# Batch 0's normalisation between layers one and two, moved into the last units of layer one and kept on chip; the first weights and rows of layer one split in pieces

## What is computed

```python
# layer one: attention over the 512 columns, 16 heads of 64, for each of 8 batches
h = concat(Wqkv0 @ z[:, :, :256] + Winj0 @ u[:, :, :256],
           Wqkv1 @ z[:, :, 256:] + Winj1 @ u[:, :, 256:])
q, k, v = split(h)
prob = softmax(((q + r_w_bias)^T k) / 8)
x = Wo @ (prob applied to v) + bo + z
m, var = mean(x, axis=1), var(x, axis=1)        # over the 256 rows
x1 = (x - m) * rsqrt(var + eps)
# layer two begins: normalisation along the 512 columns, then a recurrence
xa = (x1 - mean(x1, -1)) * rsqrt(var(x1, -1) + eps) * ln1_w + ln1_b
sx = shifted(xa) - xa
t = tanh((xa + sx * maa_x) @ maa_w1)            # then mixtures, v, g, k, r, the decay and the scan
```

## Time and profile before

| | |
|---|---|
| median of 3 runs | 3575.32 us (3566.74 to 3576.97) |
| the profiled execution's own time | 3579.84 us |
| its span in the profile | 3578.0 us |
| TensorE busy | 3336.2 us (93%) |
| VectorE busy | 2391.6 us (67%) |
| ScalarE busy | 1786.6 us (50%) |
| GpSimd busy | 193.4 us (5%) |
| DMA | 296.08 MB, mean 83 GB/s |

### The profile page before, as it was taken

One profiled execution on the slowest core, in us unless ns is written; L12 is line 12 of the kernel. 1 busy time (PEld: TensorE's weight loads), 2 busy tenths in 40 slices (PEclk: granted clock), 3 DMA queues, 4 the chain that ended last, 5 costly groups with the idle time before them and its releaser, 6 DMA issues. The chain is left out here.

```text
span 3578.0 us, 55148 instructions
## 1 busy us (share of the span) xinstructions
PE 3336.2 (93%) x21472; PEld 2557.2 (71%) x21472; DVE 2391.6 (67%) x3779; ACT 1786.6 (50%) x4253; POOL 193.4 (5%) x311
## 2 busy tenths in 40 slices
PE   7999999999999997689999999679999999699998
PEld 6777778887778875556666666357888777488885
DVE  5666666656666564399999999727777888642212
ACT  4444444444454443445655554327777777532222
POOL 0000000000000000000000000001110111000000
PEclk9999999999999998789999999779999999899999
DMA  4323311231122113354444444220011111220004
GB/s 177 118 107 130 118 72 71 89 124 71 71 95 83 71 71 117 80 117 101 105 109 113 107 107 105 55 106 1 25 40 65 48 42 37 69 71 24 24 12 160
DMA packets 93312, 296.08 MB, mean 83 GB/s; under 512 B 20000, under 2 KB 28192, under 8 KB 68480
## 3 DMA queue, kind: packets, MB, share of 16 engines
q1 hardware_dynamic: 64752, 186.47, 17.8%
q0 software_dynamic: 10368, 75.50, 5.6%
q10 hardware_dynamic: 17936, 30.59, 2.4%
HBM read 233.82 MB, written 58.72 MB: 82 GB/s over the span
## 5 line engine op out<-in xcount | busy, mean ns | idle before, releaser
L453 ACT ACTIVATE l_prob<-l_bank,l_nmax 128x512 f32<-128x512 f32 x512 | 344.9, 686 | 280.8 <-DVE l_nmax L539 280.8
L539 DVE TENSOR_REDUCE l_nmax<-l_bank 128x1 f32<-128x512 f32 x512 | 317.7, 683 | 68.4 <-PE l_bank L373 68.4
L339 PE MATMUL l_bank<-l_x_hi,l_w_hi 128*128 128x256 f32 x1024 | 297.7, 291 | 15.8 <-DVE l_x_lo L598 15.8
L562 DVE COPY l_probT<-l_bank 128x512 f32<-128x512 f32 x256 | 173.8, 689 | 178.0 <-PE l_bank L387 176.7
L339 PE MATMUL l_bank<-l_x_hi,l_w_lo 128*128 128x256 f32 x1024 | 290.8, 284 | 0.0
L339 PE MATMUL l_bank<-l_x_lo,l_w_hi 128*128 128x256 f32 x1024 | 290.7, 284 | 0.0
L1611 DVE TENSOR_TENSOR_SCAN l_kv<-l_wx,l_kv 128x2056 f32<-128x2056 f32 x64 | 283.8, 4435 | 1.9 <-DVE l_nrs L1624 1.8
L2179 ACT ACTIVATE l2a_sc<-l2a_sc,l2a_nmax 128x256 f32<-128x256 f32 x512 | 254.8, 508 | 41.1 <-DVE l2a_nmax L2295 41.1
L387 PE MATMUL l_bank<-l_ident,l_prob 128*128 128x128 f32 x2048 | 250.6, 278 | 15.2 <-DVE l_k_lo L555 10.6
L387 PEld LDWEIGHTS l_bank<-l_ident,l_prob 128*128 128x128 f32 x2048 | 229.0, 142 | 28.4 <-DVE l_k_lo L555 20.8
L409 PE MATMUL l_bank<-l_probT,l_v 128*64 128x512 f32 x1024 | 233.8, 598 | 0.0
(11 more groups left out here) (327 smaller groups left out, 8225.2 us busy)
## 6 DMA issues: line engine op xcount, KB each, us to landing
l_vb<-vd SPq DMA_DIRECT2D x64, 1024.0 KB
l_w_hi<-kept_w_hi POOLq DMA_DIRECT2D x24, 1024.0 KB, 8.2
l_w_lo<-kept_w_lo POOLq DMA_DIRECT2D x24, 1024.0 KB, 10.2
l_wv_hi<-kept_wv_hi POOLq DMA_DIRECT2D x12, 1024.0 KB, 5.1
l_wv_lo<-kept_wv_lo POOLq DMA_DIRECT2D x12, 1024.0 KB, 7.1
l_wraw<-in_l_wqk SPq DMA_DIRECT2D x8, 1024.0 KB, 8.4
kept_w_hi<-l_w_hi SPq DMA_DIRECT2D x8, 1024.0 KB, 10.9
kept_w_lo<-l_w_lo SPq DMA_DIRECT2D x8, 1024.0 KB, 12.5
```

What stands on the lines that cost most here:

```text
L339: mm = pe.matmul(s.ap[:, c * ROWS:(c + 1) * ROWS], a[:, kt, c, g, :], b[:, kt, c * ROWS:(c + 1) * ROWS], start=m == 0, stop=m == 3 * KT - 1)
L453: act.activation(prob[h][:, it, :], s.ap[:, :], ACT.Exp, bias=nmax[:, n % 2, it, h:h + 1], accum_out=rsum[:, n % 2, it, h:h + 1]).then_inc ...
L539: dve.tensor_reduce(nmax[:, n % 2, it, h:h + 1], s.ap[:, :], AX.X, ALU.max, negate=True).then_inc(max_ready, 1)
L562: dve.tensor_copy(probT[0][:, j, :], s.ap[:, :]).then_inc(s.drained, 1)
```

## The change

Thirteen small buffers of the normalisation (`an`, `x`, `own_rows`, `other_rows`, `ncol`, `bo`, `cb`, `eps`, `power`, `nrs`, `sm`, `sd`, `nb`) are allocated ahead of both layers and handed to both. Layer one makes batch 0's normalisation at the ends of its units 50 to 57: the bias product after unit 50, `centre_rows` and the two pairs of activations after 51, the variances after 52, the power on POOL in 53, the spreading and `scale_rows` after 54, the sums after 55, their power on POOL in 56, `normed` after 57. SP loads `bo` and `att[0]` after the last loads of `acc`, and stores x1 of batch 0 before the last two stores of `att`. Layer two starts with b = -1, so its first TensorE instruction is the transposes of batch 0, and loads `att[1]` in place of `att[0]`.

In layer one's start, the first weights and rows come as two halves (rows of `x`, then of `u`), each rounded and subtracted by itself; TensorE's q product starts when the first half is there and waits in front of its seventh matmul for the second. VectorE no longer waits for `rb` before the splits. In turn 0, `split_wv` moves from the lane-0 units of the odd pairs to the lane-1 units of the even pairs (units 2, 6, 10 to units 1, 5, 9).

```diff
-def l0_attention(nc, kept, d, x, u, att):
+def l0_attention(nc, kept, first, d, x, u, att, x1):
+    NORM = HALF - 14
+    BIAS, CENTRE, VAR, SPREAD, SUMMED, NORMED = NORM, NORM + 1, NORM + 2, NORM + 4, NORM + 5, NORM + 7
@@ order of the PSUM slots
+            order += {BIAS: ["cb"], CENTRE: ["nc_0", "nc_1"], VAR: ["nv"], SPREAD: ["nr"]}.get(n, [])
@@ SP, start and end of layer one
-                sp.dma_start(wraw[:, :, :, :, :], d["l0_wqk"][0]).then_inc(wraw_in, 16)
-                load_x(0, 0)
+                for h in H2:
+                    own = slice(h * RT, (h + 1) * RT)
+                    sp.dma_start(wraw[:, own, :, :, :], d["l0_wqk"][0][:, own, :, :, :]).then_inc(first_in[h], 16)
+                    sp.dma_start(xraw[:, own, :], (x, u)[h][0].rearrange("(r p) n -> p r n", p=P)).then_inc(first_in[h], 16)
...
+                sp.dma_start(bo[:, :], d["l0_bo"]).then_inc(bo_in, 16)
+                sp.wait_ge(acc_stored[0], 16)
+                sp.dma_start(an[:, :, :], att[0].rearrange("(r p) n -> p r n", p=P)).then_inc(an_in, 16)
+                sp.wait_ge(x1_ready, 1)
+                sp.dma_start(x1[0].rearrange("(r p) n -> p r n", p=P), xf[:, :, :]).then_inc(x1_stored, 16)
                 for l in range(LANES):
                     store_acc(TURNS - 1, l)
@@ TensorE
+                    if n == 0:
+                        pe.wait_ge(first_lo, 2)
...
+                            if n == 0 and name == "q" and c == 0 and m == 3 * RT:
+                                pe.wait_ge(first_lo, 4)
...
                     turn_probs(n)
                     turn_sums(n)
+                    if n == BIAS:
+                        bias_rows()
+                    if n == CENTRE:
+                        centre_rows()
+                    if n == VAR:
+                        column_variances()
+                    if n == SPREAD:
+                        spread_deviations()
@@ ScalarE
                     sums(n)
+                    if n == BIAS:
+                        bias_rows()
+                    if n == CENTRE:
+                        centred()
+                    if n == SUMMED:
+                        moments()
+                    if n == NORMED:
+                        normed()
@@ VectorE
-                dve.wait_ge(rb_in, 16)
-                split_w(0)
-                split_x(0, 0)
+                for h in H2:
+                    own = slice(h * RT, (h + 1) * RT)
+                    dve.wait_ge(first_hi, 2 * h + 1)
+                    dve.tensor_tensor(w_lo[0][:, own, :, :, :], wraw[:, own, :, :, :], w_hi[0][:, own, :, :, :].bitcast(F32),
+                                      ALU.subtract).then_inc(first_lo, 1)
...
+                dve.wait_ge(rb_in, 16)
                 split_wv(0)
...
                     if bp == 0 and l == 0 and pair + 1 < HP:
                         split_w(pair + 1)
-                        if pair % 2 == 1:
-                            split_wv((pair + 1) // 2)
+                    if bp == 0 and l == 1 and pair % 2 == 0 and pair + 2 < HP:
+                        split_wv(pair // 2 + 1)
...
                     probs(n)
+                    if n == VAR:
+                        column_deviations()
+                    if n == SPREAD:
+                        scale_rows()
@@ layer two
-    ALL = range(-2, B + 1)
+    ALL = range(-1, B + 1)
...
-                load_att(0)
-                sp.dma_start(bo[:, :], d["l0_bo"]).then_inc(bo_in, 16)
                 sp.dma_start(vec[:, :, :], d["l1_vec"]).then_inc(first_in, 16)
                 sp.dma_start(w1[:, :, :], d["l1_w1"]).then_inc(first_in, 16)
                 load_before(0)
+                load_att(1)
...
-                pe.wait_ge(consts, 2)
-                bias_rows()
+                pe.wait_ge(consts, 1)
...
-                        pe.wait_ge(xn_ready, p + 1)
+                        if p:
+                            pe.wait_ge(xn_ready, p)
```

More of the change, by code:

```diff
@@ new lines, in normed @@
+                def normed():
+                    act.wait_ge(x1_stored, 16)
+                    act.wait_ge(dev_ready, 1)
+                    for r in range(RT):
+                        ins = act.activation(nb[:, r:r + 1], nb[:, r:r + 1], ACT.Copy, scale=sd[:, r:r + 1])
+                    ins.then_inc(nb_ready, 1)
+                    act.wait_ge(nb_ready, 1)
+                    for r in range(RT):
+                        act.activation(xf[:, r, :], xf[:, r, :], ACT.Identity, bias=nb[:, r:r + 1], scale=sd[:, r:r + 1]).then_inc(xn_ready, 1)
@@ L742, with l1_layer @@
 MIX = ["w", "k", "v", "r", "g"]
-def l1_layer(nc, d, att, x1, u, vd, x2):
+def l1_layer(nc, first, d, att, x1, u, vd, x2):
     HS, NJ, PER, CG = 16, 8, 8, 32
```

209 lines of the change are left out of this document (150 added, 59 removed).

## The result

| | before | changed |
|---|---|---|
| median | 3572.51 us (3566.74 to 3576.97, 4 runs) | 3537.59 us (3535.91 to 3546.13, 4 runs) |
| ratio to before | | 0.9908, 95% interval 0.9895 to 0.992 |
| the profiled execution's own time | 3579.84 us | 3535.91 us |
| TensorE busy | 3336.2 us | 3319.9 us |

The change saves 34.9 us by the medians. A second study later gave the changed kernel 3537.57 (ratio 0.9899, 0.9882 to 0.9915).

The account below looks back on a forecast made before the run. It took TensorE to bound layer one and a chain of short steps to bound the gap behind it. -5.5 - 6.9 + 8.4 - 28.7 = -32.7 from 3575.3 gave 3542.6, rounded 3543; range 3530 to 3557.

Parts of the forecast that it names:

- the case that was given 0.62: The prediction's main case for the whole kernel: 3543 us, with its own bounds giving 3535 to 3552.
- The start, -5.5: Layer one's start: loading and splitting first weights and rows in halves saves 5.5 us, bounds 4 to 6.5.
- The first half takes the place of the 1 MB that landed by 5.62: Layer one's start: the first halves of weights and rows, together 1 MB, land by 5.62 us.
- I take half of each: Layer one's start: half-width rounding and subtraction take half of 1.91 and 2.29 us.
- its two readings of the clock: Layer one's start: clock rises 5.9 us after the first product, gain 6.1; or counted anew after the pause, gain 4.8.
- The splits, -7: Turn 0 of layer one: one split per unit instead of two saves 2.3 us per group, 6.9 over three groups.
- 1.4 us lost for one of lateness: Unit 2 of layer one: TensorE loses 1.4 us for each microsecond that `k_lo` comes late.
- rival C: Units 50 to 57: inserted waits over 4 us let TensorE's clock fall, giving 3587 us; chance 0.02.
- Added to layer one, +8.4: Layer one's late units: 7.4 us of added products plus 1.0 of stall, bounds 7.4 to 14.
- length less 2.4: Layer one: work ahead of the exponentials costs TensorE its length less 0.96 + 1.5 = 2.4 us.
- The gap, -28.7: Between layers one and two: first product with a weight at 1417.6 instead of 1446.27, saving 28.7 us, bounds 20 to 32.
- Until then its own ten issues: Layer two's start: ScalarE is busy with ten load issues until `w1` lands at 1410.8.

Follow-up runs that it names:

- the squares twice: The changed kernel with only the two squares of batch 0's sums repeated on ScalarE ahead of unit 56's exponentials; 3539.2 us (one time).
- the issues moved: The changed kernel with ScalarE's ten issues of layer two's later constants behind first_part of batch 0 instead of at its start; 3532.6 us (one time).
- the sums twice: The changed kernel with all sums of batch 0's x1, on ScalarE between units 55 and 56, made twice; 3544.3 us (one time).

## Why the prediction was right, and where it was off

The forecast was 3543, measured 3537.6, inside the range and in the case that was given 0.62. Of the 5.4 us between them, 2.8 are the level of before (3575.3 in the runs shown, 3572.5 with a fourth), 2.2 the sum, -34.9 against -32.7, and the rest rounding. That the sum came so close is in part luck: the start was put 1.6 us too high and the splits 2.1 too low, and the two cancel.

- **The start, -5.5: -3.9.** The mean of v's first product is 23.6 over the three runs with the old start and 19.7 over the eight with the change's. This is just outside the bounds of 4 to 6.5. Three steps failed. "The first half takes the place of the 1 MB that landed by 5.62": it landed at 6.43 to 6.75, the second at 9.14 to 9.86. "I take half of each" for half the width: 1.06 and 1.23, where half of 1.91 and 2.29 is 0.96 and 1.15. So the first product came at 10.03 to 10.34, forecast 9.0. And of its two readings of the clock the dearer is the right one: with a pause in front of the seventh product the half clock lasts 2.9 to 5.9 us counted from the restart, 5.5 to 8.5 from the first product; without a pause it is 2.7 to 5.9 (each to the first record under 0.36 us). That 5.9 us, the longest of the starts without a pause, was taken for the length hid that this part varies by 3 us from run to run. The Trainium skill says in the place that the prediction named ("TensorE: Matmul & The Clock Gate", on the clock's states) that the ramp differs between runs of one kernel; the thirteen profiles agree. Whether it is a budget of time and not of matmuls they can't decide, since at half clock the products stand 0.21 us apart in all of them; either has to be counted from the restart, where the prediction's 6.1 counted through the pause.
- **The splits, -7: -9.0.** That a single split is hidden for the most part was seen rightly (it costs 0.55 where 1.0 was forecast), but "1.4 us lost for one of lateness" read a fall of the clock as a slope. The rival C of the prediction priced just this mechanism, and looked for it in the new units alone, while it was at work in unit 2 of before: the term failed by a wait of 2.86 us followed by a granted 0.50.
- **Added to layer one, +8.4: +7.8.** Each product cost a little less than its row: 0.79, 3.43, 1.69, 0.90, against 1.0, 3.5, 1.9 and 1.0. The wait of unit 56 is 0.95, forecast 1.0; `centred`, `normed` and `scale_rows` were hidden, as said: units 54 and 57 are unchanged, unit 52 is longer by less than its products. The law "length less 2.4" gives 2.5 for the run with the squares twice, measured 0.95 + 1.54 = 2.49.
- **The gap, -28.7: -29.4.** The size was right and the limit not, so the size owes something to luck. "Until then its own ten issues" stood in the text as cover of `w1`; they were the limit by 1.2 us, and `w2b` came at 1411.7, in time for the product at 1412.7. The run with the issues moved shows it. Counted from layer one's last VectorE operation, `w1` and `w2b` landed at 8.3 and 15.0 where the prediction's numbers give 9.9 and 16.6, and the issues, until 9.4, took up most of the difference.
- **The rest of the layers.** Layer two's scans start 33.2 us nearer to layer one's end in this pair of profiles, where some 29 were forecast; the 3.8 beyond the gap are spread of the prologue. This prologue, from the first product with a weight to the first scan, took 56.9 to 64.4 us in the eleven profiles with the old order of v's loads, with no relation to the edits that these show (the same changed kernel took 58.1 and 62.0): in the longest (the sums twice) the granted clock is 0.54 from 10 to 20 us behind the first product, where the start alone has 1.00. From the first scan to the last VectorE operation it took 2064.9 in before and 2058.4 in the changed kernel, over the 5 us by which the prediction would have called itself wrong; but the kernel with the start alone, which has none of the moved work, took 2058.4 too, and that with the squares twice 2064.4. So these 6.5 us can't be put down to the moved work, and two single profiles of this kernel can't be subtracted to better than some us.
- **Rival C.** It was to decide from 6.4 us of ScalarE's work ahead of the exponentials. With 6.5 the clock fell, with 4.9 it didn't, and between them nothing was tried; the change's 3.35 stay clear. What it priced at 2.9 more than the wait cost 2.1, and it needed no 4 us of idle time in the record: 2.7 were enough, and in unit 63 even 2 in some executions.

The sum with the measured terms: -3.9 - 9.0 + 7.8 - 29.4 = -34.5, against -34.9 from the medians.

## What to carry to other kernels

A chain of short steps between two stages can be worth moving into a stage whose bound engine takes it at the bare length of its products; price each product by the distance of starts at full clock, and the other engines' share by the spare time ahead of the bound engine's next need. Before a stall is given a slope, look at the granted clock behind it: a long wait of TensorE (here from about 2 us on, in some executions) costs its length and more, so two extras on a helper engine are best put in different units. And once a chain is cut, look at what its first engine itself does before its first step, its own DMA issues included, and at loads queued behind a wait that they do not need.

## What the runs showed of the hardware

- TensorE's clock fell to half behind eight waits of 2.86 us, one of 3.22 and one of 2.73, and did not behind 0.66, 1.02 and 1.11. Near 2 us it did either: behind the same wait of 1.95 to 2.05 in unit 63 in seven profiles of thirteen, behind 2.12 in five. It then stayed down for 2.9 to 6.7 us of nearly unbroken work, and not equally long for the same code: twenty transposes took 4.05 us in one execution and 4.53 in another.
- At the start the half clock lasted 2.7 to 5.9 us of unbroken work in thirteen profiles, though the code in front of TensorE's first product was the same within each kind.
- Two transfers of 512 KB in half runs of the weights' memory, with the rows, landed some 0.9 us later than the whole 1 MB of weights: 6.43 to 6.75 in eight profiles, against 5.62 to 5.79 in five. That the shorter runs are the cause was not separated from the other queue neighbours.
- ScalarE's issue of a load took 0.39 to 0.73 us in the changed kernel, and `turned`, which stands behind the ten, began only when the last was over (1406.18, 1406.31). Behind activations the issues cost these nothing: in the run with them moved the first starts at 1405.85, beside the first of four activations that stand ahead of it (1405.84 to 1407.54), and these took 1.70 us as in the changed kernel. Moving them also let the loads of SyncE land sooner (`w2b` 5.8 instead of 8.0 us).
